# A hybrid attention/scan block on one core: dividing the local softmax by its sums after the values instead of before them

## The reference, cut to what matters

```
scores = einsum('bhnqd,bhnkd->bhnqk', qb, k3) / sqrt(HD) + bias
attn = softmax(scores, axis=-1)                # exp(s - max) / sum
ao = einsum('bhnqk,bhnkd->bhnqd', attn, v3)    # 32 queries x 8 channels of each head
attn_out = ao @ wo
out = x + 0.2 * attn_out + 0.45 * ssm_out + 0.15 * conv_out + 0.2 * mem_out
```

## Time and profile before

| | value |
|---|---|
| median of 3 runs | 1114.3 us |
| profiled execution | 1114.23 us |
| its span | 1112.4 us |
| DVE busy | 979.3 us (88%) |
| POOL busy | 955.6 us (86%) |
| ACT busy | 837.5 us (75%) |
| PE busy | 830.9 us (75%) |
| mean granted TensorE clock | 0.871 of 2.4 GHz |

### The profile page before, as it was taken

How to read it: one execution, slowest core, us unless ns; L and a number is a source line. 1 busy time by engine, 2 the same in 40 slices (tenths; PEclk the granted TensorE clock), 3 DMA queues, 4 the chain that set the end, 5 groups by cost and what they waited for, 6 DMA issues and landing times. The chain is left out here.

```text
span 1112.4 us, 19145 instructions
## 1 busy us (share of the span) xinstructions
PE 830.9 (75%) x4151; PEld 339.3 (30%) x4151; DVE 979.3 (88%) x2299; ACT 837.5 (75%) x2255; POOL 955.6 (86%) x675
## 2 busy tenths in 40 slices
PE   5367878688777786877778777867868778677775
PEld 2023333233323332333323333323332333232332
DVE  2688999979997999979999699897999799999991
ACT  4468886788778878687877887679887887858871
POOL 6369988989898988988899898899989898979892
PEclk9556998978997989979898798888899798989897
DMA  5845667647675666666676476665666566766630
GB/s 111 196 126 169 180 159 185 171 138 198 163 183 155 185 167 159 172 157 172 168 203 161 128 191 162 167 173 159 177 176 183 153 187 165 188 161 164 196 95 9
DMA packets 124391, 181.18 MB, mean 163 GB/s; under 512 B 29263, under 2 KB 41056, under 8 KB 124256
## 3 DMA queue, kind: packets, MB, share of 16 engines
q1 hardware_dynamic: 123968, 179.56, 61.4%
q10 hardware_dynamic: 288, 0.20, 0.1%
HBM read 170.79 MB, written 5.05 MB: 158 GB/s over the span
## 5 line engine op out<-in xcount | busy, mean ns | idle before, releaser
L1389 POOL TENSOR_TENSOR prod<-hst,C 128x1024 f32<-128x1024 f32 x256 | 602.0, 2354 | 94.9 <-DVE hst L1201 94.4
L1201 DVE TENSOR_TENSOR_SCAN hst<-decay,bank 128x512 f32<-128x512 f32 x384 | 459.5, 1209 | 3.0 <-DVE cv_a L1236 2.8
L1189 DVE TENSOR_TENSOR bank<-bank,B 128x512 f32<-128x512 f32 x384 | 263.1, 685 | 52.6 <-PE bank L911 34.8
L665 ACT ACTIVATE decay<-wide,A_rep 128x512 f32<-128x512 f32 x384 | 273.4, 715 | 41.5 <-DVE hst L1201 31.2
L911 PE MATMUL bank<-spread,sel_bc 96*128 96x512 bf16 x384 | 164.5, 434 | 101.0 <-DVE hst L1201 90.6
L679 ACT ACTIVATE prob<-s_sb,nmax 128x96 f32<-128x96 f32 x512 | 185.2, 365 | 0.9 <-DVE nmax L1214 0.5
L1405 POOL TENSOR_TENSOR uwide<-uwide,B 128x512 f32<-128x512 f32 x128 | 162.7, 1271 | 22.5 <-DMA uwide<-u_rows 22.5
L935 PE MATMUL bank<-prod,sel_red 128*32 128x512 f32 x1024 | 164.9, 722 | 0.0
L1201 DVE TENSOR_TENSOR_SCAN hst<-bank,uwide 128x512 f32<-128x512 f32 x128 | 155.4, 1214 | 2.7 <-POOL uwide L1405 2.7
L951 PE MATMUL bank<-ident,prob 128*96 128x128 f32 x512 | 85.9, 295 | 77.5 <-ACT ao L695 58.3
L944 PE MATMUL bank<-k,q 128*128 128x384 f32 x256 | 126.7, 580 | 22.3 <-DVE nmax L1214 22.2
(11 more groups left out here) (189 smaller groups left out, 1027.4 us busy)
## 6 DMA issues: line engine op xcount, KB each, us to landing
wide<-dt_rows SPq DMA_DIRECT2D x512, 256.0 KB, 4.7
uwide<-u_rows SPq DMA_DIRECT2D x128, 256.0 KB, 4.1
spread<-parts SPq DMA_DIRECT2D x66, 32.0 KB, 4.1
x_sb<-in_L_attn_x_dram SPq DMA_DIRECT2D x8, 256.0 KB, 4.5
dt_rows<-sp_t SPq DMA_DIRECT2D x8, 256.0 KB, 2.6
out_dram<-outb SPq DMA_DIRECT2D x8, 256.0 KB, 3.9
vw<-v_tok SPq DMA_DIRECT2D x80, 16.0 KB, 3.3
u_rows<-uv SPq DMA_DIRECT2D x8, 64.0 KB, 2.4
```

Source lines behind the costliest of these rows:

```text
L665: nc.scalar.activation(to, wide[m % SLOTS][:, s % 2, :], ACT.Exp, scale=A_rep[:, g:g + 1]).then_inc(exp_done, 1)
L1189: v.tensor_tensor(uP[s % 4][:, :], uP[s % 4][:, :], B2[p][:, :], ALU.mult).then_inc(dbx_done, 1)
L1201: v.tensor_tensor_scan(hst[:, s % 8, :], kept, into[:, :], 0.0, ALU.mult, ALU.add).then_inc(scan_done, 1)
L1389: g.tensor_tensor(prod[:, 2 * (m % 4):2 * (m % 4) + 2, :], hst[:, 2 * (m % 4):2 * (m % 4) + 2, :], C2[p][:, :].unsqueeze(1).to_broadcast([ ...
```

## The change

GpSimd's division of the probabilities (prob_norm) goes. The exps stay undivided through the transposes and the product with the values. ScalarE copies that product to ao_raw; TensorE transposes it (turn, lag 10) into the free columns of the bank that holds the scores, so that queries stand on partitions; VectorE multiplies 4 x 8 = 32 columns by the reciprocals (output_norm, lag 11) into ao_q. At step 63 of the batch four transposes (heads) turn ao_q back into ptP, and ScalarE copies that, times 0.2, to aoT at step 0 of the next batch (heads_copy). The projection n = 6 to 9 becomes four products of 128 columns each with weights wo4, which hold wo four times, each copy on other partitions; these are loaded by 16 DMAs behind the first window_values instead of 4 ahead of the body, and VectorE no longer scales them but clears them at the very start.

The lags become shorter: transposes at 6 instead of 9, values at 8 instead of 11, the copy at 8 instead of 11; the reciprocals move from 6 to 8. The window's DMAs move from m = 4, 5, 6 to m = 3, 4, 5. The core of the diff:

```
-LAST_PROJECT = {60: (0, 1), 61: (2, 3), 62: (4, 5), 63: (6, 7)}
+LAST_PROJECT = {60: (0, 1), 61: (2, 3), 62: (4, 5)}
-VALUE_DMA_AT = {4: (0, 1, 2, 3, 4, 5), 5: (6, 7, 8), 6: (9, 10, 11)}
+VALUE_DMA_AT = {3: (0, 1, 2, 3, 4, 5), 4: (6, 7, 8), 5: (9, 10, 11)}
-BIAS_LAG, EXP_LAG, INV_LAG, NORM_LAG, PT_LAG, PT_COPY_LAG, PV_LAG, AO_COPY_LAG = 2, (3, 4), 6, 5, 9, 9, 11, 11
+BIAS_LAG, EXP_LAG, INV_LAG, PT_LAG, PT_COPY_LAG, PV_LAG, RAW_COPY_LAG, TURN_LAG, NORM_LAG = 2, (3, 4), 8, 6, 6, 8, 8, 10, 11
+TURN_AHEAD = 3
...
-                sp.wait_ge(const_ready, 2)
-                for g in range(KVH):
-                    sp.dma_start(wo_p[32 * g:32 * g + HD, :, :],
...
+            def load_output_weights():
+                sp.wait_ge(wo_clean, 1)
+                for c in range(4):
+                    for g in range(KVH):
+                        sp.dma_start(wo4[32 * c + g * HD:32 * c + g * HD + HD, c, :, :],
+                                     wo[g * REP * HD:(g + 1) * REP * HD, :].rearrange("(r h) e -> h r e", r=REP)) \
+                            .then_inc(w_in, 16)
...
                 for at in VALUE_DMA_AT.values():
                     window_values(B, at)
+                load_output_weights()
...
-                    wait(sp, s_ready, B * NBLK + 1)
+                    wait(sp, u_ready, B * POOL_Q * GROUPS + 3)
...
+            def raw_copy(B, k):
                 wait(act, pv_ready, B * NBLK + k + 1)
+                wait(act, turned, B * NBLK + k - 1)
+                nc.scalar.activation(ao_raw[:, k % 2, :], ptP[:, 0:128], ACT.Copy).then_inc(raw_evac, 1)
+            def heads_copy(B):
+                wait(act, heads_ready, B + 2)
+                nc.scalar.activation(aoT[:, :, :, :].rearrange("p c r q -> p (c r q)"), ptP[:, :], ACT.Copy,
+                                     scale=RW_ATTN).then_inc(heads_evac, 1)
...
                 wait(pe, s_max, B * NBLK + k)
+                wait(pe, ao_norm, B * NBLK + max(0, k - TURN_AHEAD))
...
             def prob_transposes(B, k):
-                wait(pe, p_norm, B * NBLK + k + 1)
-                wait(pe, ao_evac, B * NBLK + k)
+                wait(pe, p_exp, B * NBLK + k + 1)
+                wait(pe, raw_evac, B * NBLK + k)
...
+            def turn(B, k):
+                wait(pe, raw_evac, B * NBLK + k + 1)
+                wait(pe, ao_norm, B * NBLK + k)
+                nc.tensor.transpose(sP[:, KVH * 3 * W:], ao_raw[:, k % 2, :], ident[:, :]).then_inc(turned, 1)
+            def heads(B):
+                wait(pe, ao_norm, (B + 1) * NBLK)
+                transposes([ao_q[:, 4 * a:4 * a + 4, :].rearrange("p k c -> p (k c)") for a in range(4)], 128, 128, ptP) \
+                    .then_inc(heads_ready, 1)
...
-                    ins = mm(jobP[:, :], wo_p[:, n - 6, :], ao4[:, n - 6, :], start=False, stop=False)
+                    c = n - 6
+                    for r in range(REP):
+                        ins = mm(jobP[:, :].rearrange("p (a c q) -> p a c q", a=4, c=4)[:, :, c, :], wo4[:, c, r, :],
+                                 aoT[:, :, r, :], start=False, stop=False, skip_group_check=True)
...
+            def output_norm(B, k):
+                wait(dve, turned, B * NBLK + k + 1)
+                wait(dve, p_inv, B * NBLK + k + 1)
+                wait(dve, heads_ready, B)
+                v.tensor_tensor(ao_q[:, k, :].rearrange("p (g h) -> p g h", h=HD),
+                                sP[:, KVH * 3 * W:].rearrange("p (g c) -> p g c", c=W)[:, :, 0:HD],
+                                pinv[:, k % 4, :].unsqueeze(2).to_broadcast([128, KVH, HD]), ALU.mult).then_inc(ao_norm, 1)
...
-            def prob_norm(B, k):
-                wait(pool, p_inv, B * NBLK + k + 1)
-                g.tensor_tensor(prob[:, k % 4, :, :], prob[:, k % 4, :, :],
-                                pinv[:, k % 4, :].unsqueeze(2).to_broadcast([128, KVH, 3 * W]), ALU.mult) \
-                    .then_inc(p_norm, 1)
```

More of the change, by code:

```diff
@@ L146, in hybrid_block_kernel @@
         wk_s = sb("wk_s", [D, KVH * HD])
-        wo_p = sb("wo_p", [128, REP, D])
+        wo4 = sb("wo4", [128, 4, REP, D])
         w_ssm = sb("w_ssm", [D, D])
@@ L676, in probabilities @@
                     wait(act, s_max, B * NBLK + k + 1)
[L677 removed]
+                    wait(act, pt_ready, B * NBLK + k - 1)
+                    wait(act, p_inv, B * NBLK + k - 3)
                 for g in (2 * half, 2 * half + 1):
[L679 removed]
+                    ins = nc.scalar.activation(prob[:, k % 2, g, :], s_sb[:, k % 2, g, :], ACT.Exp,
                                                bias=nmax[:, k % 2, g:g + 1], scale=-1.0,
@@ L947, in prob_transposes @@
             def prob_transposes(B, k):
-                wait(pe, p_norm, B * NBLK + k + 1)
-                wait(pe, ao_evac, B * NBLK + k)
+                wait(pe, p_exp, B * NBLK + k + 1)
+                wait(pe, raw_evac, B * NBLK + k)
+                if k == 0:
+                    wait(pe, heads_evac, B)
                 for g in range(KVH):
-                    ins = nc.tensor.transpose(ptP[0:3 * W, g * 128:(g + 1) * 128], prob[:, k % 4, g, :], ident[:, :])
+                    ins = nc.tensor.transpose(ptP[0:3 * W, g * 128:(g + 1) * 128], prob[:, k % 2, g, :], ident[:, :])
                 ins.then_inc(pt_ready, 1)
@@ L1056, in body @@
                         values(B, p, k)
+                    k = block_at(s, TURN_LAG)
+                    if k is not None:
+                        turn(B, k)
+                    if s == UNITS - 1:
+                        heads(B)
                     for tap in range(TAPS):
@@ L1073, in tail @@
             def tail(B, p):
-                for n in range(8, N_PROJ - 1):
+                for n in range(6, N_PROJ - 1):
                     project(B, p, n)
@@ L1119, in setup_step @@
                 if s == 1:
-                    dve.wait_ge(w_in, 16 * N_W_DMA)
-                    v.tensor_scalar(wo_p[:, :, :], wo_p[:, :, :], RW_ATTN, None, ALU.mult)
+                    dve.wait_ge(w_in, 16 * (N_W_DMA + N_WO_DMA))
                     v.tensor_scalar(w_ssm[:, :], w_ssm[:, :], RW_SSM, None, ALU.mult).then_inc(w_scaled, 1)
@@ L1172, in front @@
             def front(B, p):
+                v.memset(wo4[:, :, :, :], 0.0).then_inc(wo_clean, 1)
                 v.memset(ptP[:, :], 0.0).then_inc(pt_clean, 1)
@@ L1208, in scores_there @@
                 wait(dve, p_exp, B * NBLK + k - 1)
+                if k >= TURN_AHEAD:
+                    wait(dve, turned, B * NBLK + k - TURN_AHEAD + 1)
             def bias_and_max(B, k):
@@ L1289, in body @@
                         inverse_sums(B, k)
+                    k = block_at(s, NORM_LAG)
+                    if k is not None:
+                        output_norm(B, k)
                     t = memory_tile_at(s, M_MAX_LAG)
@@ L1335, in other_constants @@
             def other_constants():
-                g.memset(wo_p[:, :, :], 0.0).then_inc(const_ready, 1)
-                g.memset(k4[:, :, :], 0.0)
+                g.memset(k4[:, :, :], 0.0).then_inc(const_ready, 1)
                 for p in range(2):
@@ L1421, in body @@
                             pool_input(B + 1, 1 - p, 0)
-                    k = block_at(s, NORM_LAG)
-                    if k is not None:
-                        prob_norm(B, k)
                     if not first(B):
```

37 lines of the change are left out of this document (18 added, 19 removed).

## The result

The changed kernel takes 1199.3 us (median of 4 runs, 1197.61 to 1210.91) against 1114.8 us for the kernel before: a ratio of 1.076, with a 95% interval of 1.068 to 1.085. The prediction was 1146.3 us with a range of 1124 to 1166. The direction was right; the size, +32 us, was less than half of the measured +84.5.

What follows compares the result with a forecast made beforehand. VectorE, busy 979.3 of 1112.4 us, was taken as the bound, with a chain of three waits per batch. Terms 14.7 + 10.5 - 4.9 + 1.2 + 1.4 + 1.2 + 7 + 1 = 32.1 on 1114.2 gave 1146.3 us (1124 to 1166).

Steps and rivals of the forecast that it cites:

- The step that failed: TensorE: one added transpose per block, 0.2 us, hidden in idle time except one in the chain, +1.2 us.
- Rival 4: Worse: half clock and VectorE waiting for the turn (+7.4), multiplications of 0.18 us (+10): 1164 us; chance 0.12.
- the half clock: TensorE's clock after each 5 us standing still: VectorE loses 3.15 instead of 2.1 us per batch.
- The sign of being wrong: Profile after: vw wait under 2 us, three waits gone, or VectorE waiting for the turn in most blocks.
- The window of values: Block 0's values at step 14 wait 5 us for late DMAs; VectorE loses 2.1 us in seven batches: +14.7 us.
- the upper of the two cases: VectorE at step 17 loses 3.15 us per batch, with TensorE at half clock behind the window's wait.
- VectorE's multiplication: 128 added instructions of 32 columns at 0.10 us between starts, 12.8 us, partly hidden: +10.5 us (9 to 23).
- The cover of 22: About 22 multiplications fall between steps 18 and 28 of batches 1 to 6, where VectorE waits anyway.
- GpSimd's division: Its 0.82 us ahead of the second normalisation's root goes, in six batches: -4.9 us (0 to -10).
- the whole chain with it: ScalarE's 1.73 us wait for the root, and the chain to VectorE's three waits, shrink by 0.82 us.
- The start: Sixteen weight DMAs delay the setup chain; Gelu ends at 63.6 instead of 56.81: +7 us (4 to 10.5).
- The rest: Small TensorE and tail terms: turn in the chain +1.2, projection +1.4, later scores +1.2, tail +1 us.

Runs made afterwards that it cites:

- the kernel with the turn mended: Changed kernel with the turn issued 9 steps behind the scores instead of 10 and right behind them in its TensorE step; window and start unchanged: 1142.9 us.
- the last rung: Changed kernel with turn at lag 9 and right behind the scores, window DMAs behind pairs 1 and 2, output-weight DMAs behind pair 14 of the first batch: 1112.5 us.

## Why the prediction was wrong, by its own steps

**The step that failed** is the sentence "The turns themselves fall in TensorE's idle time elsewhere". It counted the turn as work (0.2 us) and not as something that VectorE waits for at the head of a step. The diff has the wait in `scores_there`, a whole input multiplication and scan ahead of the multiplication that uses the turn, and this wait was put at nothing. Rival 4 named "VectorE waiting for the turn", but its 7.4 us are seven times the 1.05 us of the half clock, so it gave the turn no price either. What the runs showed in its place: the turn's place is worth 56.4 us with the late window in the kernel (1199.3 to 1142.9). The sign of being wrong, VectorE waiting for the turn "in most blocks", nearly came: 47 waits of L1229 and 5 of L1241 for 128 blocks.

**The window of values**: right mechanism, under-sized. The wait of 5 us, its place and the half clock behind it came as forecast. VectorE lost 3.4 us a batch by it (23.8 us over seven in the kernel with the turn mended), not the middle value of 2.1; its edit gives 24.4 us against the predicted 14.7. The reduction of 1.94 us and the scores of 1.65 us are both at the lower clock, so the upper of the two cases (3.15) was the one to take after 5 us without work. In the changed kernel the turn behind the scores made it 34.4.

**VectorE's multiplication**: +16 (6 to 24) against 10.5, which the time can't tell apart. The distance between starts was well read: 0.08 us measured against 0.10, and 12.0 us more of busy time for 128 in the kernel before (13.6 in the changed one) against 12.8. The cover of 22 was not seen: VectorE's idle time over batches 1 to 7 is 73.1 us with the multiplications and 70.5 without. The Trainium skill's formula (VectorE: DVE Perf Modes, section "The TRN2 errata — SBUF-src ops pay a fixed extra latency per instruction") led to an estimate of 0.19 us each and 24 us in all. The trace does not agree: an instruction lasts 0.163 us, and what 128 add to the busy time is half of that estimate. The prediction's own 1157 us by that formula doesn't go with its term of 24 either, which in place of 10.5 would give 1160.

**GpSimd's division**: forecast -4.9. The time alone (-6 to +4 us) doesn't exclude it, but VectorE's idle sum fell by only 1.1 us. The root did come 0.77 us earlier, but "the whole chain with it" was wrong: shortening the first link moved the waits along.

**The start**: 5.3 and 6.0 us against 7. The size was about right and the reason was not: the prediction said of the wide DMAs that they "are there first", while the exp, behind which the Gelu stands, waits 2.02 us for one of them in the changed kernel too, and the setup chain's own wait adds nothing. The Gelu ended at 61.13 us instead of the forecast 63.6.

**The rest** (turn in the chain, projection, later scores, tail, 4.8 us together) was not measured term by term. One of its sums is off: 14 times 0.17 us for the later scores are 2.4 us, not 1.2. The projection at the end takes 3.84 us instead of the 3.70 of the earlier trace rows. The rest cannot be large in sum: the last rung, with all of it and +16 for the multiplications, takes as long as the kernel before. Something must even give back some 18 us there. In the profiles VectorE is busy 12.3 us more (991.6 against 979.3), and its idle sum is 12.6 us lower: 16.5 less at steps 24 to 26 and 3.7 less at steps 1 to 16 and at 33 to 64 each, 8.4 more at steps 19 to 23 and 2.3 more at 27 to 32. No run here separates the shorter lags from the rest, so the cause stays open.

The sum of the mended terms: 1114.8 + 16 (multiplications) + 6 (start) + 24.4 (window) + 56.4 (turn's place) = 1217.6 us, 18 us above the measured 1199.3; these 18 are the open part just named, and as uncertain as the 16. For the same reason it is luck that the kernel with only the turn mended took 1142.9 us, so near the predicted 1146.3: the measured terms add up to 1161, 15 us above the forecast, and the gain of 18, which was not forecast, takes that back.

## What to carry to other kernels

A new product that is written beside an old one in a shared bank makes the readers of the old one wait for the new one too. Price that wait where the reader first stands, not where the product is used, and put the new instruction directly behind the one that is waited for in any case. A position in an in-order queue can cost far more than the instruction: here 0.3 us of transpose, placed one step late, cost 39 us, and 56 together with its place behind other work in the step. And when a chain of waits is explained by its first link, ask what each engine in it has to do anyway; here the first link was shortened in one run and taken away in another, and neither changed the time in a way that could be told.

## What was not expected of the hardware

A small multiplication of VectorE with both operands in SBUF waited out whatever GpSimd was doing: 128x32 took 738 ns at the median and up to 2326 ns, against 165 and 181 ns with one operand in PSUM, while GpSimd was busy 80% of the span; all 100 long ones ended with a GpSimd instruction. The Trainium skill (SBUF — State Buffer, section "Who interferes with whom") says that a VectorE instruction with two SBUF inputs contends with a GpSimd instruction that reads SBUF, for a port pair that works as "an exclusive lock". The trace agrees with it. It also means that the change was right to let VectorE read the turned output in PSUM, although the shared bank brought the costly wait.
